# A graph-network block with routed experts on one core: a lighter barrier, two loads moved to ScalarE, other paces for the routing and later second weights

## What is computed

```python
xn = layernorm(x)
# 1. graph attention with 8 heads: softmax over the incoming edges of each node
ea = leaky_relu(s_src[src] + s_dst[dst]); ea = softmax_by_destination(ea)
gnn = segment_sum(h[src] * ea, dst)
# 2. a mixer: attention over channels, and an MLP (gelu)
x = x + gnn + mix(xn)
# 3. eight experts, the best two of each node by the gate
probs = softmax(layernorm(x) @ gate_w + gate_b)
out = x + sum over the best two experts e of probs[e] * (gelu(xf @ W1[e] + b1[e]) @ W2[e] + b2[e])
```

## Time and profile before

| | |
|---|---|
| median of 3 runs | 3237.46 us (3234.16 to 3254.78) |
| profiled execution, its time | 3240.78 us |
| profiled execution, its span | 3239.5 us |
| mean granted TensorE clock | 0.919 of full speed |
| busy share of the span | TensorE 82%, GpSimd 69%, VectorE 62%, ScalarE 48% |
| barrier 2, about | 2345 us from the start of the span |

### The profile page before, as it was taken

The page is one execution under the profiler, slowest core; times in us unless marked ns, Lnnn a source line. Parts: engine busy times, 40 slices in busy tenths (PEclk is TensorE's granted clock), DMA queues, the critical chain, the costliest instruction groups (busy, mean ns, idle before and its releaser), DMA issues.

```text
span 3239.5 us, 42164 instructions
## 1 busy us (share of the span) xinstructions
PE 2646.1 (82%) x11525; PEld 2052.0 (63%) x11525; DVE 2015.4 (62%) x5482; ACT 1553.4 (48%) x3392; POOL 2236.9 (69%) x2187
## 2 busy tenths in 40 slices
PE   7657776888898888988899886564578999999998
PEld 6546555666675666656566564442357887878887
DVE  7445567667676777767677676787554555445422
ACT  5325544555554556545465454343344545445444
POOL 0277777777777777777777777777557766776644
PEclk9879988999999999989999898887789999999999
DMA  8797766566566666666656666556666666666663
GB/s 274 245 297 210 198 176 171 162 173 179 164 172 178 175 178 169 166 179 173 178 164 170 178 163 175 161 156 191 217 177 160 155 156 160 151 143 127 139 109 61
DMA packets 397718, 561.17 MB, mean 173 GB/s; under 512 B 71976, under 2 KB 318030, under 8 KB 397305
## 3 DMA queue, kind: packets, MB, share of 16 engines
q0 software_dynamic: 123696, 298.61, 36.3%
q1 hardware_dynamic: 196457, 170.61, 18.0%
q10 hardware_dynamic: 77255, 88.59, 9.9%
HBM read 402.43 MB, written 169.68 MB: 177 GB/s over the span
## 4 chain that ended last, share of the span: by engine, by line
PE 65%; DMA 10%; ACT 9%; issue 6%; DVE 5%; POOL 5%; ACTq 1%; SPq 0%; DVEq 0%; POOLq 0%
PE bank L1447 21%; PE bank L2494 10%; PE bank L2507 9%; PE bank L1179 7%; DMA rows<-table,srcix 7%; PE bank L1168 5%; POOL rows L1364 4%; PE bank L1141 2%; PE bank L684 1%; PE bank L685 1%; PE bank L949 1%; ACT L1488 1%; DMA last_d<-fout 1%; ACT L1284 1%; ACT e_hn L2085 1%
## 5 line engine op out<-in xcount | busy, mean ns | idle before, releaser
L1364 POOL DMA_INDIRECT rows<-table,srcix x1536 | 1476.4, 961 | 468.1 <-issue 333.4
L1447 PE MATMUL bank<-rows,onehot 128*128 128x272 f32 x3328 | 921.6, 424 | 56.3 <-ACT fout L1504 51.9
L1504 ACT ACTIVATE fout<-bank 128x272 f32<-128x272 f32 x1659 | 638.6, 397 | 589.1 <-PE bank L1447 541.9
L1447 PEld LDWEIGHTS bank<-rows,onehot 128*128 128x128 f32 x3328 | 661.3, 206 | 239.7 <-ACT fout L1504 77.9
L1601 DVE TENSOR_TENSOR rows<-rows,bank 128x1024 f32<-128x1024 f32 x416 | 483.7, 1212 | 171.8 <-ACT rows L1493 171.3
L2585 POOL DMA_INDIRECT out<-x_y,x_dest x203 | 326.3, 1607 | 244.1 <-DMA out<-x_y,x_dest 157.3
L2494 PE MATMUL bank<-x_int,x_w1c 128*128 128x256 f32 (+1 forms) x1696 | 380.5, 378 | 23.0 <-issue 19.7
L2507 PE MATMUL bank<-e_w,x_ht 128*128 x1624 | 373.9, 383 | 8.4 <-issue 6.2
L2494 PEld LDWEIGHTS bank<-x_int,x_w1c 128*128 128x128 f32 x1696 | 317.5, 195 | 74.2 <-issue 32.2
L2533 ACT ACTIVATE x_ht<-bank,x_b1c 128x256 f32<-128x256 f32 (+1 forms) x424 | 172.9, 462 | 392.1 <-PE bank L2494 391.9
L2507 PEld LDWEIGHTS bank<-e_w,x_ht 128*128 128x128 f32 x1624 | 302.8, 192 | 51.3 <-issue 13.8
(11 more groups left out here) (461 smaller groups left out, 3405.6 us busy)
## 6 DMA issues: line engine op xcount, KB each, us to landing
frag<-fout ACTq DMA_DIRECT2D x104, 544.0 KB
x_in<-sorted_d SPq DMA_DIRECT2D x97, 260.0 KB
rows<-table,srcix POOLq DMA_INDIRECT x1536
x_b2c<-in_L_ffn_b SPq DMA_DIRECT2D x106, 128.0 KB, 3.6
frag<-in_x ACTq DMA_DIRECT2D x1, 13416.0 KB
table<-hr SPq DMA_DIRECT2D x24, 544.0 KB, 4.0
xs<-in_x SPq DMA_DIRECT2D x24, 512.0 KB, 6.1
xg<-in_x SPq DMA_DIRECT2D x24, 512.0 KB, 6.0
```

What stands on the lines that cost most here:

```text
L1364: p.indirect_dma_start(out=B.rows[b][:, j, :], out_offset=None, in_=B.table[:, :], in_offset=bass.IndirectOffsetOnAxis(ap=chunk_columns(B. ...
L1447: pe.matmul(B.banks[2 + c % 3][:, 0:ROW], B.onehot[k % 2][:, j, :], B.rows[k % NR][:, j, :], start=True, stop=True).then_inc(S.sum, 1)
L1504: a.activation(B.fout[k % 2][:, j, :], B.banks[2 + c % 3][:, 0:ROW], ACT.Copy).then_inc(S.ev, 1)
```

## The change

Five edits. `MEET[2]` goes from 10 to 9 and GpSimd's `reach` after its gathers goes. The last entry of the schedule beside the edges has 23 steps fewer due (`PLAN` is 6), so VectorE's indices 97 to 119 of round 1 run after group 103, in `beside.rest()`. In the last merge SyncE issues `second_weights` after it has waited for the merge's sums. ScalarE issues the node loads of rounds 2 and 3 right behind barrier 2, where SyncE did behind t = 4 (round 4's stay there). And `lead` is 2, 5, 8, 11, 12, 12, ... for rounds 2, 3, 4, 5, 6, ...

```diff
-MEET = {1: 5, 2: 10}
+MEET = {1: 5, 2: 9}
...
-            (FIRST_FROM + 4, first + routing)]
+            (FIRST_FROM + 4, first + routing - PLAN - 17)]
...
-            second_weights(sp, S, B)
-        yield from idle(MERGE_STEPS - 1)
-        if not final:
+        yield from idle(MERGE_STEPS - 1)
+        if final:
+            sp.wait_ge(S.mg_sum, 3 * (w + 1))
+            second_weights(sp, S, B)
+        else:
             sp.wait_ge(S.mg_sum, 3 * (w + 1))
             sp.dma_start(ends[p0:p0 + n, b0:b0 + m, :], first[0:n, 0:m, :]).then_inc(S.mg_out, 16)
...
-def fetch_nodes(sp, S, B, r):
+def fetch_nodes(e, S, B, r):
...
     def steps(r):
-        if r == FIRST_ROUNDS:
-            fetch_nodes(sp, S, B, r)
-            fetch_nodes(sp, S, B, r + 1)
         if r >= FIRST_ROUNDS and r + 2 < len(ROUNDS):
             fetch_nodes(sp, S, B, r + 2)
...
-    lead = lambda r: 2 if r == FIRST_ROUNDS else EARLY * (1 + (r == len(ROUNDS) - 1))
+    lead = lambda r: min(EARLY, 2 + 3 * (r - FIRST_ROUNDS)) * (1 + (r == len(ROUNDS) - 1))
...
     edges_pool(p, S, B, range(GROUPS))
-    reach(p, S)
     for _ in route_pool(p, S, B, FIRST):
...
     barrier(a, S, 2)
+    for r in (FIRST_ROUNDS, FIRST_ROUNDS + 1):
+        fetch_nodes(a, S, B, r)
     late(route_scalar(a, S, B, LATER), experts_scalar(a, S, B))
```

More of the change, by code:

```diff
@@ L1985, in sorted_rows @@
     return x.rearrange("(p t) d -> p t d", t=SUB)
-def fetch_nodes(sp, S, B, r):
+def fetch_nodes(e, S, B, r):
     if r >= NF:
-        sp.wait_ge(S.e_x1[r % NF], stored_to(r - NF))
-        sp.wait_ge(S.e_hn, R_FIRST[r - NF] + R_TILES[r - NF])
+        e.wait_ge(S.e_x1[r % NF], stored_to(r - NF))
+        e.wait_ge(S.e_hn, R_FIRST[r - NF] + R_TILES[r - NF])
     for k in ROUNDS[r]:
@@ L1994, in fetch_nodes @@
         o = s - R_FIRST[r]
-        sp.dma_start(B.e_x[r % NF][:, o:o + n, :], rows_of(B.xm_d, s, n)).then_inc(S.e_x[r % NF], 16)
+        e.dma_start(B.e_x[r % NF][:, o:o + n, :], rows_of(B.xm_d, s, n)).then_inc(S.e_x[r % NF], 16)
 def first_sync(sp, S, B):
```

## The result

The change is slower by about half a per cent. The median of nine runs is 3260.56 us (3251.51 to 3265.31), beside 3240.31 us of the kernel before in the same session; the ratio is 1.0054 [1.0037, 1.0071]. The profiled execution took 3253.67 us (span 3252.3), 12.9 us more than the profiled one of before. The trace can account for these 12.9 us; the other 7 us between the medians are not in it.

The account below looks back on a forecast made before the run. The prediction took TensorE to bound the kernel from 2600 us on. It summed +1.4 us through round 2, -8.0 at round 4 and -2.0 at rounds 5 and 6 to -8.6: 3232.2 profiled, 3229 us as median, range 3216 to 3243.

Parts of the forecast that it names:

- Edits 1 and 2: Ahead of barrier 2: dropping GpSimd's drain gives 0 us; moving 23 steps wins TensorE's 2.57 us, first fetch 5.0 us late.
- Edit 3: Barrier 2: second weights behind the merge's sums delay the first rows; TensorE's first tile 9.5 us late (5 to 16).
- I take 2360.5: Landing time of the first expert rows, chosen a little under the middle of the bounds 2355.9 and 2367.
- the fetch ... stands behind these weights: After barrier 2: the first fetch, issued at 2351.5 on SyncE's queue, waits behind the 4.2 MB of second weights.
- Edit 4: Round 2's turn: node loads on ScalarE remove the 5.86 us wait; the clock staying up wins 1.8 and 0.9 us.
- Edit 5: Paces: round 3's 8.45 us stay; round 4's waits go, -8.0 us; rounds 5 and 6 give -2 us.
- From round 7 on all is as before: Later rounds: claimed no change, so that gains won in earlier rounds reach the kernel's end.
- Rival 1: First rows not held up by the weights, landing 4.4 us behind issue; 9.5 becomes 5, 3224.5 us; chance 0.22.
- Rival 2: Late first tile: fetch behind 4.2 MB sharing DMA engines with loads and sends, held to 2375; 3243.5 us; chance 0.15.
- Rival 3: Round 4: VectorE's work needs more than 16 places, so the -8 becomes -2; 3235 us; chance 0.13.
- Rival 4: Change does not do what it says: drain hides nothing, 5.86 us stay at round 2; 3235 us; chance 0.05.
- the signs listed for a wrong prediction: Sends done before the barrier, TensorE starting by 2352 or after 2369, or over 3 us waits at round 3/4 fetches.

Follow-up runs that it names:

- run 4: Kernel before with only round 1's last 23 VectorE steps moved behind group 103; 3246.28 us, ratio 1.0000 to before.
- run 14: The changed kernel with the first biases' load put ahead of the second weights; 3260.47 us, ratio 1.0036 to before.
- run 10: Kernel before with the second weights issued after the last merge's sums, by ScalarE instead of SyncE; 3249.16 us, ratio 1.0025 to before.
- run 7: Kernel before with only the node loads of rounds 2 and 3 given to ScalarE behind barrier 2; 3242.33 us, ratio 1.0000 to before.
- run 12: Kernel before with one output add left out of each tile having two, plus the change's `lead`; 3215.93 us, ratio 0.9916 to before.
- run 1: Kernel before with only the change's new `lead`; 3253.77 us, ratio 1.0024 to before.
- run 2: The changed kernel with the old `lead` (2, 12, 12 ...); 3249.52 us, ratio 1.0024 to before.
- run 11: Kernel before with one output add left out of each expert tile that has two; 3231.27 us, ratio 0.9969 to before.
- run 5: Kernel before without GpSimd's drain, node loads on ScalarE, 17 steps of round 1 moved behind group 103; 3248.63 us, ratio 1.0004 to before.
- run 6: Kernel before with only the second weights issued late, by SyncE behind the last merge's sums; 3257.60 us, ratio 1.0044 to before.
- run 9: Kernel before without GpSimd's drain, node loads on ScalarE, 16 steps of round 1 moved behind group 103; 3233.17 us, ratio 0.9973 to before.
- run 3: The changed kernel with round 1's last 23 steps back ahead of group 102; 3257.35 us, ratio 1.0038 to before.

## Why the prediction was wrong

The forecast was 3229 us, 8.6 us less than before; measured were 13 to 20 us more.

**Edits 1 and 2** were sized rightly in their sum: the drain is worth nothing, the wait of 2.57 us goes, and run 4 gives edit 2 as nothing. Within it there is some luck. The sends end at 2344.4 (2346.6 on before's clock; 2348.4 forecast), but those around them land 5.0 us behind their issue, not the 2.8 of the earlier trace rows, and so the fetch is issued at 2352.1 on before's clock, where 2351.5 was forecast. The row at 2304.62 is the 15th of round 0's sends and not its last; round 1's begin at 2307.15, with the same 1.27 us each, and no term changes.

**Edit 3** has the first failed step: "I take 2360.5", 9.0 us behind the fetch's issue, from bounds of 2355.9 and 2367 that counted only large bytes. The first tile came at 2366.83, 16.9 us behind the issue and 2369.0 on before's clock, outside the bounds. Run 14 splits this. Without the small packets 12.9 us are left, so the choice between the bounds was 3.9 us too low; and 4.0 more are the load that stands between barrier and fetch, 4096 small packets, which the sum did not hold. Its row at 2345.28 shows an issue of 0.39 us and nothing of them; it landed 16 us later than in before. That it matters on whose queue the weights are ("the fetch ... stands behind these weights" on SyncE's) was argued and is refuted by run 10.

**Edit 4**: round 2's wait went and the clock stayed up (16 matmuls in 3.62 us), as forecast. What the step lacked is the price of 2.1 MB in the engines just when the biases and the first rows are wanted, 9 us at the first tile (run 7). Alone it comes out even.

**Edit 5** was right in its mechanism and in kind for rounds 4 and 5; the gain was larger than forecast (15 us between tiles 4 and 11, run 12: 15.3, forecast 8 + 2). The second failed step is "From round 7 on all is as before", with the sentence "TensorE has no slack behind these places, so what is won there reaches the end". The runs show in its place that 13.7 us of the gain are gone by tile 47, and that edit 5 alone loses 0.24% (run 1) where with half of the adds it wins 15.3 us. TensorE's busy 189 of 200 us was read as the only bound. GpSimd's 143 of 200 us looks like room, but its waits for an add to land and the 0.3 us between its issues are not idle time that it could use: in 700 us it waited for VectorE 16. A row for that was to be had before the run.

The two steps together make the miss. Edits 1 to 4 cost 0.24% by themselves (run 2), and edit 5 costs 0.24% by itself (run 1); the change costs 0.54%.

**Rivals.** Rival 1 is refuted: the first rows come 16.9 us behind their issue. Rival 2 named the right sign and place but not enough: the late tile alone (4.3 us left behind round 2) would have been covered by edit 5's gain. Rival 3 is refuted, both of round 4's waits went. Rival 4 is refuted, each edit does what it says; its 3235 us is also not its own sum, which with "-2.7 + 5" gives 3240. The bulk of the loss came by a way that no rival named, and none of the signs listed for a wrong prediction covers it: the first tile was before 2369 in its own execution, and the waits at the fetches of rounds 3 and 4 stayed under 1.7 us.

The last 5 us are in the tail: VectorE's last scaling ends 7.3 us later than in before, and GpSimd's last add starts 14.5 us behind that end instead of 9.3. In runs 11 and 12 it starts 2.0 us behind. What stays open is which part of an add (its issue, its bytes, its landing) makes the bound, how much of an earlier first tile reaches the end, and the 7 us by which the medians differ more than the two profiled executions.

## What to carry to other kernels

Before a gain at the bounding engine is counted, ask of the next engine not how busy it is but how long it waits for the bounding one; if that is next to nothing, the gain only fills the buffers between them and is paid back when the ring is full. Count a transfer by its packets too: a load of 16 KB in single elements belongs far ahead of any barrier, and not between two large queues and the first transfer that an engine waits for. Here that was worth 2 to 7 us at the first tile, and nothing that a time shows clear of noise. And loads moved away from one place cost at another where the DMA engines are full already.

## What had not been expected of the hardware

- 16 KB in 4-byte elements took 4.4 us with little beside it, 11.1 to 15.3 us beside one stream of 512 KB loads (runs 5, 6, 7, 9, 10), and 20.1 to 21.6 us beside two and GpSimd's indirect transfers (the change, runs 2 and 3).
- The next transfer of the same engine is held in its issue while they stand there (up to 15.7 us against 0.39), and SyncE issues nothing else meanwhile. It makes no difference to this whose queue the large loads are in (7.34 us in run 6, 8.21 in run 10). The Trainium skill, page "DMA: Bandwidth & Descriptors", section "Issuing engines are not separate DMA queues", has all of them end on the same 16 engines, and these two runs agree.
- An indirect add into the output takes GpSimd 1.6 us and a send 1.0, with 0.3 between two; two adds a tile, 16 sends and 8 fetches a round fill its time at 67 to 72% busy (2400 to 3000 us in before), as the waits for an add to land take 104 of 700 us beside them.
